# A fused Mamba, expert and attention kernel on one TensorE: the softmax maximum subtracted by transpositions, the global-score units planned side by side, and a new order

## The reference, cut to what matters

```python
x = L0_attn_x                                   # (16, 256, 128) float32
xn = _layernorm(x)
x = x + mamba(xn) + experts(xn)                 # scan with 16 states; top-1 of 8 experts
xn = _layernorm(x)
x = x + arccos_attention(xn) + two_window_layers(xn)
# arccos_attention: 16 heads of 8; cos = q k^T of normalised rows, clipped to +-(1 - 1e-7),
#   score = (1 + arccos(cos)) ** -3.2, normalised by row and column sums
# a window layer: h = shift_token(x)            # second half of the features from the token before
#   8 heads of 64, local_attention: windows of 64 that also see the window before,
#   attn = softmax(where(mask, -max, q k^T)); x += (attn v) @ wo;
#   then shift_token, layer norm, gated GELU of width 341
```

## Time and profile before

| | |
|---|---|
| median of 3 runs | 2231.05 us (2231.03 to 2246.01) |
| profiled execution | 2229.43 us, span 2227.9 us |
| TensorE busy | 1918.6 us (86%) |
| VectorE busy | 1749.3 us (79%) |
| ScalarE busy | 1716.7 us (77%) |
| GpSimd busy | 606.3 us (27%) |
| mean granted TensorE clock | 0.892 |

### The profile page before, as it was taken

The page is one execution under the profiler, slowest core; times in us unless marked ns, Lnnn a source line. Parts: engine busy times, 40 slices in busy tenths (PEclk is TensorE's granted clock), DMA queues, the critical chain, the costliest instruction groups (busy, mean ns, idle before and its releaser), DMA issues.

```text
span 2227.9 us, 37707 instructions
## 1 busy us (share of the span) xinstructions
PE 1918.6 (86%) x13746; PEld 1454.8 (65%) x13746; DVE 1749.3 (79%) x2649; ACT 1716.7 (77%) x2817; POOL 606.3 (27%) x272
## 2 busy tenths in 40 slices
PE   3677988989897889898889987899789989899997
PEld 2564766778575667667666666667666767676776
DVE  4889897675899889869976799779987898856553
ACT  2446787838887478897888989887888787897987
POOL 2351222222231033421242223403233132313221
PEclk9788888999998988999888998999889998898989
DMA  7651112442111111011200121011100111000000
GB/s 238 223 181 54 48 57 72 131 144 69 59 63 48 49 44 57 30 40 48 67 17 4 49 62 53 11 53 39 62 11 11 62 54 48 1 1 6 1 1 6
DMA packets 67687, 126.74 MB, mean 57 GB/s; under 512 B 8852, under 2 KB 40276, under 8 KB 67380
## 3 DMA queue, kind: packets, MB, share of 16 engines
q1 hardware_dynamic: 61808, 113.19, 16.2%
q0 software_dynamic: 2816, 7.21, 0.9%
q10 hardware_dynamic: 2884, 3.93, 0.5%
HBM read 111.46 MB, written 12.85 MB: 56 GB/s over the span
## 4 chain that ended last, share of the span: by engine, by line
PE 39%; DVE 25%; issue 17%; ACT 14%; DMA 2%; SPq 2%; POOL 0%; DVEq 0%; another core or an unknown queue 0%; ACTq 0%; POOLq 0%
PE ps L815 6%; DVE hB L1536 5%; PE ps L1063 4%; PE ps L1123 3%; DVE hB L1530 3%; PE ps L1159 2%; DVE hB L1542 2%; PE ps L1195 2%; ACT L810 2%; PE ps L1013 2%; PE ps L1166 2%; PE ps L1165 2%; DVE lss L1659 2%; DVE rb L1666 2%; ACT arena L1374 2%
## 5 line engine op out<-in xcount | busy, mean ns | idle before, releaser
L1823 POOL TENSOR_TENSOR arena<-arena 128x1024 f32<-128x1024 f32 x128 | 345.8, 2724 | 755.9 <-ACT arena L1353 755.8
L1827 POOL TENSOR_TENSOR arena<-arena,rb 128x1024 f32<-128x1024 f32 x64 | 166.2, 2596 | 672.0 <-DVE rb L1666 672.0
L1536 DVE TENSOR_TENSOR_SCAN hB<-dA,hB 128x1024 f32<-128x1024 f32 x128 | 316.7, 2479 | 0.7 <-ACT dA L1312 0.5
L815 PE MATMUL ps<-w_ident,arena 128*128 128x128 f32 x879 | 158.4, 333 | 104.9 <-DVE arena L1469 30.7
L815 PEld LDWEIGHTS ps<-w_ident,arena 128*128 128x128 f32 x879 | 127.5, 173 | 136.3 <-issue 81.2
L1374 ACT ACTIVATE arena<-arena 128x256 f32<-128x256 f32 x512 | 205.4, 402 | 2.0
L1312 ACT ACTIVATE dA<-mv,w_A_log 128x510 f32<-128x510 f32 x256 | 168.5, 712 | 49.3 <-DVE hB L1536 48.6
L1123 PE MATMUL ps<-w_l_wqkv,arena 128*128 128x512 f32 x384 | 196.3, 640 | 10.5 <-DVE nmx L1684 6.2
L810 ACT ACT_TABLE_LOAD x147 | 188.6, 1283 | 15.3 <-issue 12.7
L1530 DVE TENSOR_TENSOR hB<-BC,mv 128x1024 f32<-128x1024 f32 x128 | 189.3, 1483 | 13.8 <-PE ps L1013 10.8
L1607 DVE TENSOR_SCALAR arena<-ps 128x1024 f32<-128x1024 f32 x128 | 155.2, 1217 | 40.6 <-PE ps L1063 40.5
(11 more groups left out here) (222 smaller groups left out, 4554.6 us busy)
## 6 DMA issues: line engine op xcount, KB each, us to landing
BC<-bc_d SPq DMA_DIRECT2D x128, 512.0 KB
BC<-in_experts SPq DMA_DIRECT2D x16, 514.0 KB
arena<-in_experts SPq DMA_DIRECT2D x15, 514.0 KB
mv<-in_experts SPq DMA_DIRECT2D x15, 514.0 KB, 3.6
arena<-in_x SPq DMA_DIRECT2D x8, 256.0 KB, 5.6
xnT_d<-arena SPq DMA_DIRECT2D x8, 256.0 KB, 4.9
hB<-xnT_d SPq DMA_DIRECT2D x8, 256.0 KB
x<-in_x SPq DMA_DIRECT2D x8, 256.0 KB, 4.0
```

Source lines behind the costliest of these rows:

```text
L815: return t.transpose(out_, in_, ident[0:k, 0:k])
L1536: v.tensor_tensor_scan(hf, flat2(dA[k % 2]), hf, 0.0, ALU.mult, ALU.add).then_inc(v_scan, 1)
L1823: g.tensor_tensor(la[m % 2][:, half], la[m % 2][:, half], cl[m % 2][:, half], ALU.subtract).then_inc(g_sub, 1)
```

## The change

Four things. (1) In `pt` the float32 products with the identity become transpositions that accumulate, three of 128 columns for each head; the mask grows from 320 to 384 columns, and `ident_q` goes. (2) The planner knows that a `g_score` unit directly behind another one is shorter (`BESIDE`) and prefers it (`PAIR`), and that entering `g_score` or `g_av` from other work costs something (`TILE_SWITCH`). (3) The `shift` unit's copies move from ScalarE to VectorE, with the semaphore `v_hT` for `a_hT`. (4) Lengths, `LANDS`, `CLOCK`, `SWITCH` and all due times are new, so the order of units on all engines is.

```diff
-    "shift": [("PE", 0.22), ("ACT", 0.97)], ...
-    "score": [("PE", 1.0), ("DVE", 0.61)], "pt": [("PE", 2.32), ("ACT", 0.7)], ...
+    "shift": [("PE", 0.22), ("DVE", 0.75)], ...
+    "score": [("PE", 1.0), ("DVE", 0.68)], "pt": [("PE", 1.75), ("ACT", 0.7)], ...
-LANDS = {"PE": 0.27, "ACT": 0.12, "DVE": 0.12, "SP": 4.5, "POOL": 0.15}
+LANDS = {"PE": 0.27, "ACT": 0.21, "DVE": 0.2, "SP": 4.5, "POOL": 0.15}
-CLOCK = 0.88
+CLOCK = 0.85
+OVERLAP = {"ACT": 0.09, "DVE": 0.08}
+TILED, TILE_SWITCH, BESIDE, PAIR = ("g_score", "g_av"), 0.11, 0.6, 150.0
-SWITCH = 127.0
+SWITCH = 182.0
 ...          # LATER, STREAM: every value is new
@@ def durations(unit)
-        return [("PE", 0.11), ("DVE", 0.22)]
+        return [("PE", 0.11), ("DVE", 0.28)]
-        return [("PE", 0.89), ("DVE", 0.82)]
+        return [("PE", 0.89), ("DVE", 1.12)]
@@ def stages(unit)
-    return [(e, time / CLOCK if e == "PE" else time) for e, time in durations(unit)]
+    return [(e, time / CLOCK if e == "PE" else time - OVERLAP.get(e, 0.0)) for e, time in durations(unit)]
@@ def schedule()
+                    if e == "PE" and unit[0] == "g_score" == tile:
+                        cost -= PAIR
...
+                if e == "PE":
+                    if unit[0] in TILED and unit[0] != tile:
+                        takes += TILE_SWITCH
+                    elif unit[0] == "g_score":
+                        takes -= BESIDE
+                    tile = unit[0]
@@ tensor_program, pt
-                        t.matmul(lb(z)[:, 0:SC], ident_b[:], maskT_b[:], start=True, stop=False)
+                        t.matmul(lb(z)[:, 0:3 * P], ident_b[:], maskT_b[:], start=True, stop=False)
...
-                        t.matmul(lb(z)[:, 0:P], top[0], ident, start=False, stop=False)
-                        e = t.matmul(lb(z)[:, P:SC], top[1], ident_q[:], start=False, stop=True)
+                        t.matmul(lb(z)[:, 0:P], top[0], ident, is_transpose=True, start=False, stop=False)
+                        t.matmul(lb(z)[:, P:2 * P], top[1], ident, is_transpose=True, start=False, stop=False)
+                        e = t.matmul(lb(z)[:, 2 * P:3 * P], top[1], ident, is_transpose=True, start=False, stop=True)
@@ scalar_program, shift
-                    a.activation(hT1[b][0:64], lb()[0:64, 0:L], ACT.Copy)
-                    a.activation(hT1[b][64:128, 0:1], one_b[64:128, 0:1], ACT.Copy, scale=0.0)
-                    a.activation(hT1[b][64:128, 1:L], lb()[64:128, 0:L - 1], ACT.Copy).then_inc(a_hT[b], 1)
@@ vector_program, shift
+                    v.wait_ge(p_sh[b], n + 1)
+                    if n:
+                        v.wait_ge(p_pt[b], 4 * n)
+                    v.tensor_copy(hT1[b][0:64], lb()[0:64, 0:L])
+                    v.memset(hT1[b][64:P, 0:1], 0.0)
+                    v.tensor_copy(hT1[b][64:P, 1:L], lb()[64:P, 0:L - 1]).then_inc(v_hT[b], 1)
```

More of the change, by code:

```diff
@@ L73 @@
     "g_out": [("PE", 0.89), ("DVE", 0.68)], "out": [("DVE", 0.69), ("SP", 0.1)], "zeros": [("DVE", 0.34)],
-    "shift": [("PE", 0.22), ("ACT", 0.97)], "norm": [("DVE", 0.17), ("ACT", 0.5)], "qn": [("DVE", 1.22)], "heads": [("PE", 0.88), ("ACT", 1.03)],
-    "score": [("PE", 1.0), ("DVE", 0.61)], "pt": [("PE", 2.32), ("ACT", 0.7)], "pv": [("PE", 0.64)], "on": [("DVE", 0.78)],
+    "shift": [("PE", 0.22), ("DVE", 0.75)], "norm": [("DVE", 0.17), ("ACT", 0.5)], "qn": [("DVE", 1.22)], "heads": [("PE", 0.88), ("ACT", 1.03)],
+    "score": [("PE", 1.0), ("DVE", 0.68)], "pt": [("PE", 1.75), ("ACT", 0.7)], "pv": [("PE", 0.64)], "on": [("DVE", 0.78)],
     "oT": [("PE", 0.44), ("ACT", 0.6)], "wo": [("PE", 1.83), ("DVE", 0.42)], "ln": [("PE", 0.69), ("DVE", 0.77), ("ACT", 0.54)],
@@ L101 @@
-STREAM = {("e", 0): 131, ("e", 1): 87, ("e", 2): 61, ("e", 3): 65, ("e", 4): 580, ("e", 5): 193, ("e", 6): 235,
[13 rows of a table removed]
+SWITCH = 182.0
+LATER = {"down": 174, "e_down": 55, "e_lg": -299, "e_ln": 133, "e_load": -2161, "e_place": 264, "e_pre": 171, "e_route": -1026,
+         "e_scat": 381, "e_store": -1391, "e_tr": 906, "e_up": -151, "e_xn": -324, "e_xt": -246, "f_ln": 109, "f_tr": -807,
+         "f_xn": 146, "f_yg": 1204, "g_av": 101, "g_avT": -955, "g_ev": -1170, "g_hd": -26, "g_ln": 1491, "g_norm": -237,
+         "g_oT": 124, "g_out": 480, "g_pow": 425, "g_qkv": 95, "g_score": 67, "g_sq": 139, "g_sub": 1891, "g_tan": 101, "gelu":
+         -171, "heads": 11, "hid": -568, "l_weights": 266, "ln": -114, "ln2": -232, "lnT": -27, "m_B": 822, "m_C": -1190,
+         "m_bx": 9, "m_dt": -81, "m_du": 517, "m_ex": -40, "m_fin": 88, "m_hc": 83, "m_in": -268, "m_load": -295, "m_out":
+         -1246, "m_scan": 1484, "m_sum": -4, "m_turn": -203, "m_weights": -2232, "m_xp": 1328, "norm": -73, "oT": -188, "on":
+         -170, "out": 2, "pt": -87, "pv": 54, "qkv": 15, "qn": -653, "score": 13, "shift": -493, "up": -437, "wo": -62,
+         "x_load": -747, "zeros": -70}
@@ L116 @@
+STREAM = {("e", 0): 216, ("e", 1): -61, ("e", 2): -71, ("e", 3): 240, ("e", 4): 466, ("e", 5): 130, ("e", 6): 294,
[13 rows of a table added]
 LOADED = [15.0, 24.0]
@@ L407, in schedule @@
     taken = set()
-    table = "ln"
+    table, tile = "ln", ""
     dual_until = pool_until = 0.0
@@ L609, in build @@
         rot = load("rot", [P, LAY, 2, 2, 2, LD])
-        ident_q = sb("ident_q", [P, SC - P])
-        mask_b, maskT_b = sb("mask_b", [P, SQ], BF16), sb("maskT_b", [P, SC], BF16)
+        mask_b, maskT_b = sb("mask_b", [P, SQ], BF16), sb("maskT_b", [P, 3 * P], BF16)
         ident_b = sb("ident_b", [P, P], BF16)
@@ L744, in build @@
         zero = a0.get(DM)
-        mask, maskT = PT[0][:, 0, 0:SQ], PT[1][:, 0, 0:SC]
+        mask, maskT = PT[0][:, 0, 0:SQ], PT[1][:, :, 0:3 * P // 2]
         qks = a0.get(LAY, 2, 2, LD)
-        first += [(w_before, d["before"]), (gate, d["gateT"]), (rank, d["rank"]), (mask, d["mask"]), (maskT, d["maskT"])]
+        first += [(w_before, d["before"]), (gate, d["gateT"]), (rank, d["rank"]), (mask, d["mask"]), (maskT, d["maskT"].rearrange("p (h c) -> p h c", h=2))]
         later.append((qks, d["qk_scale"]))
@@ L780, in build @@
         p_avT, v_go, a_goT, p_go, v_ho = sem("p_avT"), sem("v_go"), sem("a_goT"), sem("p_go"), sem("v_ho")
-        p_sh, a_hT, p_q, v_rot, a_sq, v_sq, a_v, g_rb = (sem2("p_sh"), sem2("a_hT"), sem2("p_q"), sem2("v_rot"), sem2("a_sq"), sem2("v_sq"),
+        p_sh, v_hT, p_q, v_rot, a_sq, v_sq, a_v, g_rb = (sem2("p_sh"), sem2("v_hT"), sem2("p_q"), sem2("v_rot"), sem2("a_sq"), sem2("v_sq"),
                                                        sem2("a_v"), sem2("g_rb"))
@@ L899, in vector_setup @@
             v.tensor_copy(mask_b[:], mask)
-            v.tensor_copy(maskT_b[:], maskT)
-            v.tensor_copy(ident_q[:, 0:P], ident)
-            v.tensor_copy(ident_q[:, P:], ident[:, 0:WIN])
+            v.tensor_copy(maskT_b[:].rearrange("p (h c) -> p h c", h=2), maskT)
             v.tensor_copy(ident_b[:], ident).then_inc(v_set, 1)
@@ L1114, in tensor_program @@
                     e.then_inc(p_sh[b], 1)
-                    read_by(unit, a_hT[b], n + 1)
+                    read_by(unit, v_hT[b], n + 1)
                 elif u == "qkv":
@@ L1118, in tensor_program @@
                         t.wait_ge(d_w, all_w)
-                    t.wait_ge(a_hT[b], n + 1)
+                    t.wait_ge(v_hT[b], n + 1)
                     tt, w = divmod(k, 3)
@@ L1162, in tensor_program @@
                     for z in range(2):
-                        hh = 2 * (k % 2) + z
-                        top = [bc(nmx[b][:, hh, qt:qt + 1], [P, P]) for qt in range(2)]
-                        t.matmul(lb(z)[:, 0:P], top[0], ident, start=False, stop=False)
-                        e = t.matmul(lb(z)[:, P:SC], top[1], ident_q[:], start=False, stop=True)
+                        top = [bc(nmx[b][:, 2 * (k % 2) + z, qt:qt + 1], [P, P]) for qt in range(2)]
+                        t.matmul(lb(z)[:, 0:P], top[0], ident, is_transpose=True, start=False, stop=False)
+                        t.matmul(lb(z)[:, P:2 * P], top[1], ident, is_transpose=True, start=False, stop=False)
+                        e = t.matmul(lb(z)[:, 2 * P:3 * P], top[1], ident, is_transpose=True, start=False, stop=True)
                         read_by(unit, a_pt[b], 4 * n + k + 1, z)
@@ L1649, in vector_program @@
                     v.tensor_tensor(ho, ho, xd, ALU.add).then_inc(v_ho, 1)
+                elif u == "shift":
+                    v.wait_ge(p_sh[b], n + 1)
[4 more added lines that the diff above has]
+                    v.tensor_copy(hT1[b][64:P, 1:L], lb()[64:P, 0:L - 1]).then_inc(v_hT[b], 1)
                 elif u == "qkv" and k % 3 == 0:
@@ L1986, in constants @@
     q0 = np.arange(P)[None]
-    for name, ahead in (("mask", (m0, m1)), ("maskT", (q0 - i, q0 - i, q0[:, 0:WIN] + P - i))):
+    for name, ahead in (("mask", (m0, m1)), ("maskT", (q0 - i, q0 - i, q0 + P - i))):
         d_ = np.concatenate(ahead, 1)
```

## The result

The changed kernel takes 2257.58 us at the median (2253.41 to 2262.81, 4 runs), the kernel before 2231.04 us beside it. The ratio is 1.011, 95% interval 1.0067 to 1.0152. The forecast was 2162 us, range 2110 to 2210: it is slower by 1.1% where 3% faster was forecast. The profiled execution took 2262.81 us, its span is 2261.2.

What follows compares the result with a forecast made beforehand. TensorE, busy 1918.6 of 2227.9 us, was taken as fullest, with three queues leaning on each other. Its work falls 62 + 19 = 81 us, 0.85 arrives: 69 us off 2229.4 gives 2160, plus 1.6 for the median: 2162, range 2110 to 2210.

Steps and rivals of the forecast that it cites:

- Local prices: Costs per piece: pt net 0.43 us less a unit at full clock, shift copy 0.413 us, g_score neighbour 0.56 us less.
- How much arrives: Share of TensorE's 81 us cut that reaches the kernel's end: 0.85 taken, 69 us; low end 0.45, high end 1.
- Dividing by the mean clock: In pt, 0.43 us a unit at full clock divided by 0.892 gave 0.48 us, 62 us for 128 units.
- Rival (d): Transpositions in pt don't hold TensorE's clock up, kernel ends slower, at 2255 us; sign: clock under 0.854; chance 0.06.
- Neighbours: g_score units directly behind one another on TensorE: 30 new ones, 0.63 us each at the mean clock, 19 us saved.
- The order: New due times for the units on all engines: taken at 0, with ends of -40 and +30 us.
- The shift: Copies of 32 shift units: 24 us off ScalarE, 26 us onto VectorE; taken at 0, with the end at +17 us.
- VectorE takes over, (b): While scans run VectorE bounds: 2200 us; sign: TensorE's standing time grows as much as its work shrinks; chance 0.19.

Runs made afterwards that it cites:

- the bench: Kernel before with a stretch added behind its end where TensorE alone runs transpositions, then products; granted clock 0.96 for 400 transpositions and 0.96 for 200 products.

## Why the prediction was wrong, point by point

- *Local prices.* Right: 0.43 us a `pt` unit, 0.41 us a copy, some 0.55 us a neighbour. So 55 us of work left `pt`, as worked out.
- *How much arrives.* This step failed. I let 0.85 of 81 us arrive and gave 0.45 as the low end. The runs show 0 for the transpositions (0.9995 in the old order, no difference in the new), and less than 0 for a larger cut. Two things take it back: of 53 us of work 31 by more time at the lower clock, and 34 us by longer standing. With 32 rows in `g_score` 11 us of the same cut arrive, a fifth. The low end should have gone below nothing.
- *Dividing by the mean clock.* This was the root of the clock's part. I used 0.892 as a constant of the kernel, worth 0.05 us more for each unit removed. It moves with what TensorE does: 0.892, 0.874 and 0.845 for 1711, 1658 and 1629 us of work (busy time times clock) in one order. Why it falls with the work is shown in part, by the rows of `g_score`; the rest is open.
- *Rival (d).* It named the outcome (2255 us; its price was a clock of 0.842 with 309 us standing, and 0.875 with 362 was enough, so its sign, under 0.854, never came) at a chance of 0.06, and tied it to the kind of instruction. The earlier trace rows refuted that rightly, and I took the refutation for the whole question. The Trainium skill ("TensorE: Matmul & The Clock Gate", "Part 4: PE-mode transpose") says that the full clock doesn't engage in transpose mode; the bench has 0.96 for 400 of them in one go and does not agree. The rule pointed to the right end for a reason that is not this kernel's.
- *Neighbours.* 8 came, not 30: 5 us for 19.
- *The order.* Taken at 0. With all the new work it is 0 as far as the runs tell; with all the old work it costs 49 us (2290.88 against 2241.97), beyond my end of +30. It has 12 more table loads. That its units' lengths don't fit those on the chip would explain it, which is argued and not shown.
- *The shift.* Taken at 0 with an end at +17. 12 us dearer in the old order, no more than noise with 32 rows, and 34 us cheaper in the new order with the old products. It has no price of its own apart from the order.
- *VectorE takes over, (b).* It took a part, and its sign came: TensorE's standing grew by 52.5 us while its work shrank by some 49 (1711 to 1899.4 x 0.875 = 1662). A cut of VectorE's own work pays more than a third.

What stays open is how the loss of 1.1% splits: the transpositions contribute none by themselves, so it lies in the order and the shift's move together, and the two mixed runs (1.007 for all the new work in the old order, 1.0214 for all the old work in the new) show that work and order depend on each other.

## What to carry to other kernels

Don't price a TensorE cut at a fixed clock: compute the time at the lower level, 2 x (1 - clock) x span, and allow for its growing once the work is gone. Leaving work out in one unchanged order is the cheapest test of what an engine's time is worth; here it would have said "less than nothing" for TensorE, more than a third for VectorE and a fifth for ScalarE. Products on few rows are the first to look at: wider ones, with zeros, cost no column here and gave 0.5% to 1.7%.

## What the runs showed of the hardware

- TensorE never idle for 54.9 us on products of 8 rows, clock 0.50; the same for 32 rows in two row groups; 0.93 for 64 rows and 0.94 for 128 with the engine idle a sixth of the time (one execution).
- In the kernel before, the clock fell from 1.00 to 0.50 at 805.3 us without a pause of TensorE, behind two `g_score` units on 8 rows; at the same place with 32 rows, zeros in 24 of them, it stayed at 1.00 and the next four instructions took 1.93 us for 3.63.
- Float32 transpositions and products of the same length have the same granted clock, within 0.01, at four densities (one execution).
- Taking some 95 us of full-clock work from TensorE in one unchanged order made the kernel 1.8% slower; 24 more rows of zeros in `g_score`'s products made the changed one 1.7% faster.
